# A decoder layer on one core: probability transposes by DMA instead of TensorE, in five pipeline stages

## The reference

```python
# self attention, on layernorm(x): q . (q @ anomaly) / sqrt(256)
scores = jnp.einsum('bsh,bth->bst', q, tq) / jnp.sqrt(jnp.float32(HIDDEN))
probs = jax.nn.softmax(scores, axis=-1)
ctx = jnp.einsum('bst,bth->bsh', probs, v)
return ctx * input_norm
# cross attention, on layernorm of the sum so far
attn = jnp.einsum('bhnd,bhmd->bhnm', q, k) * SCALE
attn = jnp.where(mask[:, None, :, :], attn, -jnp.inf)
attn = jax.nn.softmax(attn, axis=-1)
out = jnp.einsum('bhnm,bhmd->bhnd', attn, v)
# experts: idx = argmax(x @ Wg + bg); y = gelu(x @ W1[idx] + b1[idx]) @ W2[idx] + b2[idx]
```

## Time and profile before

| | us |
|---|---|
| median of 3 runs | 844.0 (843.88 to 845.4) |
| span of the profiled execution | 848.8 |
| TensorE, VectorE, ScalarE, GpSimd busy | 755.1, 653.2, 457.9, 138.9 |
| first and last x1 (start) | 115.0, 610.9 |
| experts' first matmul (start) | 706.8 |

### The profile page before, as it was taken

How to read it: one execution, slowest core, us unless ns; L and a number is a source line. 1 busy time by engine, 2 the same in 40 slices (tenths; PEclk the granted TensorE clock), 3 DMA queues, 4 the chain that set the end, 5 groups by cost and what they waited for, 6 DMA issues and landing times. The chain is left out here.

```text
span 848.8 us, 19493 instructions
## 1 busy us (share of the span) xinstructions
PE 755.1 (89%) x6136; PEld 681.1 (80%) x6137; DVE 653.2 (77%) x1619; ACT 457.9 (54%) x922; POOL 138.9 (16%) x246
## 2 busy tenths in 40 slices
PE   3988799999999999999999999999986416999996
PEld 2778689989889899898898998988975314999995
DVE  5984647788888888888888888888878465777773
ACT  2544626566566665666666656666665432334332
POOL 3100110120211201202112012021120410222221
PEclk9999989999999999999999999999978856999999
DMA  6242110010101000000010000000123260111110
GB/s 211 70 138 70 47 29 7 24 29 15 29 12 28 28 6 28 24 16 28 12 28 28 6 28 24 17 28 12 54 113 99 101 235 26 36 39 39 37 33 15
DMA packets 25525, 39.32 MB, mean 46 GB/s; under 512 B 3086, under 2 KB 18704, under 8 KB 25360
## 3 DMA queue, kind: packets, MB, share of 16 engines
q1 hardware_dynamic: 23232, 33.02, 12.5%
q0 software_dynamic: 2256, 5.83, 2.0%
HBM read 28.82 MB, written 10.41 MB: 46 GB/s over the span
## 5 line engine op out<-in xcount | busy, mean ns | idle before, releaser
L1076 ACT ACTIVATE ps_cross<-flip 128x512 f16<-128x512 f32 (+1 forms) x256 | 125.0, 514 | 116.5 <-PE flip L795 91.0
L1318 DVE TENSOR_TENSOR ps_cross<-flip,ps_cross 128x512 f16<-128x512 f32 (+1 forms) x256 | 145.0, 583 | 24.8 <-ACT ps_cross L1076 20.4
L795 PE MATMUL flip<-ident,exp_cross 128*128 128x128 f32 (+1 forms) x832 | 131.8, 282 | 9.9 <-DVE ps_cross L1318 6.5
L1277 ACT ACTIVATE exp_cross<-exp_cross,xneg 128x1024 f32<-128x1024 f32 (+1 forms) x128 | 122.7, 960 | 19.2 <-DVE xneg L1492 19.1
L784 PE MATMUL scores<-keys_cross,qt 128*128 128x402 f32 x512 | 127.6, 372 | 5.3 <-DVE xneg L1492 3.5
L795 PEld LDWEIGHTS flip<-ident,exp_cross 128*128 128x128 f32 (+1 forms) x832 | 95.8, 143 | 18.1 <-DVE ps_cross L1318 8.3
L672 PE MATMUL scores<-keys_self,u_tile 128*128 128x512 f32 x384 | 102.2, 403 | 6.4 <-issue 4.9
L806 PE MATMUL cross_out<-vals_cross,ps_cross 128*128 128x128 f16 (+1 forms) x832 | 102.5, 224 | 5.5 <-issue 4.9
L771 PE MATMUL flip<-vals_self,ps_self 128*128 128x256 f32 x768 | 103.8, 289 | 0.0
L806 PEld LDWEIGHTS cross_out<-vals_cross,ps_cross 128*128 128x128 f16 (+1 forms) x832 | 76.4, 101 | 28.3 <-issue 20.4
L771 PEld LDWEIGHTS flip<-vals_self,ps_self 128*128 128x128 f32 x768 | 96.7, 194 | 0.0
(11 more groups left out here) (207 smaller groups left out, 1189.2 us busy)
## 6 DMA issues: line engine op xcount, KB each, us to landing
w_stage<-W SPq DMA_DIRECT2D x8, 1024.0 KB, 5.4
u_dram<-u_out SPq DMA_DIRECT2D x4, 1024.0 KB, 5.9
u_tile<-u_dram SPq DMA_DIRECT2D x16, 256.0 KB, 2.7
mask_tile<-mask SPq DMA_DIRECT2D x16, 200.1 KB, 2.4
rows<-rows_dram SPq DMA_DIRECT2D x19, 130.0 KB, 2.1
x_all<-x SPq DMA_DIRECT2D x4, 512.0 KB, 5.8
x_tile<-x SPq DMA_DIRECT2D x16, 128.0 KB, 2.0
b_row<-b SPq DMA_DIRECT2D x1, 2048.0 KB, 8.9
```

What stands on the lines that cost most here:

```text
L795: tr = pe.transpose(flip[0:rows, bank(use), n * P:(n + 1) * P], exp_cross[:, h % 2, m * P:m * P + rows], ident[:, :])
L1076: return act.activation(out, in_, ACT.Copy, **kw)
L1277: act.activation(exp_cross[:, h % 2, cols], exp_cross[:, h % 2, cols], ACT.Exp, bias=xneg[:, h % 2, 1:2], scale=-1.0, accum_out=xden[:, ha ...
L1318: return dve.tensor_tensor(out, full, hi, ALU.subtract)
```

## The change

All float32 pieces that TensorE turned are now turned by DMA in their two float16 parts. The high part (`cross_hi`, `self_hi`) is made by ScalarE in SBUF before the turn, the low part in SBUF too: for cross heads 2, 3 and 0 on GpSimd (`low_cross`), for head 1 and both self halves on VectorE. SyncE issues 8 transposes of 128x1664 (416 KB) and 4 of 128x1024 (256 KB) per tile, 4352 KB together. The loop has five stages (`stages(k)`) and runs for j = 0 to 19: `a` is self scores of tile j, `s` self values, x1 and queries of tile j-1, `b` cross scores of tile j-2, `c` its later values and output (as j-3), `d` gate, rank and store of tile j-4. Self scores keep their four banks; cross scores use `flip` banks 0 and 1, one half head at a time; all small products share bank 2 (`SMALL`). The self values are float16 with a scale (`self_v`), the cross keys one copy with the queries in two parts, the mask's bias is made in two halves, and the expert weights are loaded and split in passes T to T+3.

```diff
+    def stages(k):
+        return k < T, 1 <= k <= T, 2 <= k <= T + 1, 3 <= k <= T + 2, k >= 4
...
+        def turn_cross(t, h, part):
+            if part == 0:
+                sp.wait_ge(cross_p_hi, H * t + h + 1)
+            else:
+                sp.wait_ge(cross_p_lo[h], t + 1)
+            sp.dma_start_transpose(out=cross_pt[:, h, part, :, :], in_=cross_p[:, h % 2, part, :]).wait_op(
+                constants_set, CONSTANTS, "sem-ge").then_inc(cross_turned[h], 16)
...
+        def body(j, k):
+            a, s, b, c, d = stages(k)
+            if c:
+                for h in (2, 3):
+                    for part in range(2):
+                        turn_cross(j - 3, h, part)
...
+            if b:
+                for h in (0, 1):
+                    for part in range(2):
+                        turn_cross(j - 2, h, part)
...
+            if a:
+                for half in range(2):
+                    for part in range(2):
+                        turn_self(j, k, half, part)
...
+        def low_cross(t, h):
+            pool.wait_ge(cross_p_hi, H * t + h + 1)
+            pool.tensor_tensor(cross_p[:, h % 2, 1, 0:MP], exp_cross[:, h % 2, :], cross_p[:, h % 2, 0, 0:MP],
+                               ALU.subtract).then_inc(cross_p_lo[h], 1)
...
-        def self_flip(j, k, g):
...
-                tr = pe.transpose(flip[:, bank(use), n * P:(n + 1) * P], exp_self[:, m * P:(m + 1) * P], ident[:, :])
...
+        def self_values(j, k, half):
+            pe.wait_ge(self_turned[half], 32 * j)
...
+            if half:
+                pe.wait_ge(cross_max_half, H * t + h + 1)
+            elif h or k > 2:
+                pe.wait_ge(cross_max_ready, H * t + h)
...
-        def cross_flip(j, k, h, g):
...
+        def cross_values(t, first, h):
+            pe.wait_ge(cross_turned[h], 32 * (t + 1))
...
+        def cross_hi(t, first, h):
...
+            copy(cross_p[:, h % 2, 0, 0:MP], exp_cross[:, h % 2, :]).then_inc(cross_p_hi, 1)
...
+        def cross_lo(t, h):
+            dve.wait_ge(cross_p_hi, H * t + h + 1)
+            low(cross_p[:, h % 2, 1, 0:MP], exp_cross[:, h % 2, :], cross_p[:, h % 2, 0, 0:MP]).then_inc(cross_p_lo[h], 1)
...
+            low(self_p[:, 1, at], exp_self[:, at], self_p[:, 0, at]).then_inc(self_p_lo, 1)
...
+                if h >= 2:
+                    dve.wait_ge(cross_p_lo[h - 2], t + 1)
+                elif k > 2:
+                    dve.wait_ge(cross_p_lo[h + 2], t)
...
-            if k == T:
-                weights_lo(0)
...
+            if k == T + 1:
+                weights_lo(0)
...
+            if k == T + 2:
                 weights_lo(2)
+                weights_lo(3)
...
+            if k == T + 3:
+                weights_lo(4)
+                weights_lo(5)
```

More of the change, by code:

```diff
@@ L44 @@
 V_TOP = 4096.0
-XHALF = 2 * 512
+SELF_V_TOP = 32768.0
+SELF_P_TOP = 16384.0
 RING = 4
 NOBODY = 65536.0
-NG = -(-MC // 4)
-XG = [range(4 * g, min(4 * g + 4, MC)) for g in range(NG)]
-BANKS = {("x", 2, 2): 0, ("x", 2, 3): 1, ("xn",): 2, ("x", 3, 0): 0, ("xq",): 2, ("qs",): 2,
[4 rows of a table removed]
[L64 to L70, removed]
+SMALL = 2
+PW = MC * P
+EARLY = 5
+STAGES = 4
 def build(nc, io):
@@ L465, in _, with turn_self, loads_w @@
         loads_a(0)
-        loads_x(0)
         sp.wait_ge(prologue_done, 3)
[L469 to L486, removed]
+        def turn_cross(t, h, part):
[5 more added lines that the diff above has]
+                constants_set, CONSTANTS, "sem-ge").then_inc(cross_turned[h], 16)
+        def turn_self(j, k, half, part):
+            at = slice(half * N // 2, (half + 1) * N // 2)
+            to = slice(half * T // 2, (half + 1) * T // 2)
+            sp.wait_ge(self_p_lo if part else self_p_hi, 2 * j + half + 1)
+            if k >= 1 and part == 0:
+                sp.wait_ge(self_p_used, 2 * j)
+            sp.dma_start_transpose(out=self_pt[:, part, to, :], in_=self_p[:, part, at]).wait_op(
+                constants_set, CONSTANTS, "sem-ge").then_inc(self_turned[half], 16)
+        def loads_w(n):
             e = n % E
@@ L798, in cross_values @@
-        def cross_values(j, k, h, g):
-            t = j - (2 if (h, g) in ((2, 0), (2, 1)) else stage_of(("x", h, g)))
-            pe.wait_ge(cross_p_lo, 16 * t + 4 * h + g + 1)
-            if h == 0 and g == 0 and k >= 2:
-                pe.wait_ge(o_summed, t)
-            for n, m in enumerate(XG[g]):
-                rows = P if m < MC - 1 else MLAST
-                pe.matmul(cross_out[:, h * P:(h + 1) * P], ps_cross[0:rows, g, 0, n * P:(n + 1) * P],
+        def cross_values(t, first, h):
+            pe.wait_ge(cross_turned[h], 32 * (t + 1))
+            if h == 0 and not first:
+                pe.wait_ge(o_summed, t)
+            for m in range(MC):
+                rows = P if m < MC - 1 else MLAST
+                pe.matmul(cross_out[:, h * P:(h + 1) * P], cross_pt[0:rows, h, 0, m, :],
@@ L995, in body @@
-            if c:
-                pe.wait_ge(x3t_ready, j - 1)
-                small(("gate",), j, k, x3t_ready, j - 1, gate_ready, gate)
+            if s:
+                small(xt_lo, j, q_ready,
+                      lambda out: three(out[:, 0:D], lambda a, c: xt[:, a, c, :], lambda b, c: wq_cross[:, b, c, :]))
+            if b:
+                cross_values(j - 2, k == 2, 0)
+            if c:
+                if s:
+                    pe.wait_ge(q_copied, j)
+                elif d:
+                    pe.wait_ge(rank_used, j - 3)
+                small(o_ready, j - 2, o_flipped, flip_row(o_tile[:, :, :].rearrange("p h d -> p (h d)")))
@@ L1025, in _ @@
+            if c:
+                if s:
+                    pe.wait_ge(qt_lo, j)
+                small(ot_lo, j - 2, wo_ready,
+                      lambda out: three(out[:, 0:D], lambda a, c: ot[:, a, c, :], lambda b, c: wo_cross[:, b, c, :]))
         run_pipeline(pe, body)
@@ L1521, in body @@
+            if d:
+                destination(j, k)
             if a:
@@ L1646, in body @@
[L1646 to L1655 removed]
+            if k == T + 2:
+                weights_lo(2)
+                weights_lo(3)
```

813 lines of the change are left out of this document (347 added, 466 removed), and 4 rows, old and new, of the table BANKS.

## The result

The changed kernel takes 928.5 us (median; 927.84 to 929.91) against 843.96 for the kernel before: 1.100 times as long, 95% interval 1.0975 to 1.1026. The forecast was 908 (848 to 980), slower.

What follows compares the result with a forecast made beforehand. A cycle through VectorE, GpSimd and TensorE was taken to set the changed loop's period at 35.5 us. In us: 848.8 + 7 (first x1) + 19 (loop) + 20 (tail) + 18 (clock) - 4.8 (offset) = 908, range 848 to 980.

Steps and rivals of the forecast that it cites:

- The cycle's steps: Loop: seven steps in line from one tile's x1 to the next, 34.8 us, or 35.5 with subtractions at 3.3.
- Step 2: Loop: VectorE's run up to cross_max of (3, 0), including cross_lo of head 1 and output work, 7.7 us.
- Step 5: Loop: GpSimd's power, mask half, subtractions of heads 2 and 3, copies and norm_col, 8.5 us with 3.07 per subtraction.
- The clock's term: Loop: TensorE's lowered clock in front of waiting engines costs 1.2 us per tile, 18 for 15 gaps; 0 to 40.
- steps 3 and 7: Loop: next scores and ScalarE's qt copy, 1.7 us; scores of (1, 0), 24 self values and hand-over, 3.8 us.
- 19 + 18: Loop: gaps of 21, 32.5 and 13 times 35.5 us, less 495.9, give 19; the lower clock adds 18.
- The prologue's term: Before the loop: first x1 about 7 us later, behind high and low parts, two transposes and all 48 values.
- The tail's term: After the last x1: one more stage, about 10 us, and the experts' weights' split, some 10; together 20.
- The offset: Whole kernel: 4.8 us subtracted because the profiled span stood that much above the median.
- The rival "faster": Loop: subtraction near 1.54 us and blocked steps falling beside others; 820 us for the kernel, chance 0.13.
- step 4: Loop: qt low, three small ones, two self_lo, cross_max (3, 1) and record's four operations, 5.7 us.
- that rival: Loop: GpSimd's subtraction at 4.2 to 5.0 us, or cross_lo and self_lo held too; 950 to 985 us, chance 0.11.

Runs made afterwards that it cites:

- run 1: The changed kernel with its three low_cross subtractions moved from GpSimd to VectorE, each ahead of the cross_max that waits for it: 896.3 us, 1.061.
- run 2: The changed kernel with GpSimd's three subtractions covering 402 of 1608 columns: 870.5 us, 1.031.
- run 5: The changed kernel with only the high parts turned, 6 DMA transposes per tile instead of 12: 918.9 us, 1.087.
- run 3: The changed kernel with gates parts 1 and 2 placed after cross_max (1, 0) in VectorE's order: 921.2 us, 1.091.
- run 6: The changed kernel with the prologue's GpSimd partition_all_reduce replaced by a memset of a fixed bound: 918.2 us, 1.087.
- kernel 8: The changed kernel with run 6's memset, new orders on VectorE and TensorE, and all three subtractions on VectorE: 822.9 us, 0.975.
- run 10: kernel 8 with only the high parts turned, 6 of 12 DMA transposes per tile: 817.6 us, 0.969.
- run 11: kernel 8 with the subtraction of head 3 back on GpSimd, those of heads 2 and 0 on VectorE: 831.5 us, 0.984.
- kernel 7: kernel 8's memset and new orders on VectorE and TensorE, but with the three subtractions on GpSimd: 907.0 us, 1.073.

## Why the prediction was right, and which terms were off

- **The cause** was the one forecast: a cycle through VectorE, GpSimd and TensorE, not the work of one engine. Run 1 moves GpSimd's part to VectorE, which was busier already, run 2 shortens it, and they gain 32 and 58 us; run 5 takes away half of the transposes and gains 2 of 538 us in the loop. That the time came out within the range is in part luck, as the terms show.
- **The cycle's steps**, predicted with 3.3 us for a subtraction and measured from 446.24: 1, 5.2 and 5.3 (to 451.54); 2, 7.7 and 8.4 (to 459.91); 3, 1.7 and 1.7; 4, 5.7 and 5.7 (to 467.34); 5, 9.0 and 9.6 (to 476.98); 6, 2.4 and 2.5 (to 479.51); 7, 3.8 and 4.0. The sum is 37.3 instead of 35.5. Step 2 was mis-sized: `xn` was not in it as held. It ends at 451.70, two small operations of the rank stand behind it, and so `cross_max` (2, 0) starts at 452.04, 0.5 us after GpSimd's subtraction. Step 5 has hand-overs and 0.39 us of waiting for ScalarE's copy.
- **GpSimd's subtraction**, taken as 3.3, is 3.26 us. The Trainium skill ("GPSIMD Engine Reference") gave 3.53 by an estimate; the row is 8% below.
- **The clock's term** of 18 us was wrong in its cause. The clock did fall to 0.51, but in steps 4 and 5, beside GpSimd's chain; steps 3 and 7, which the term was for, ran at 1.00 in the tile shown (459.91 to 461.64 and 479.51 to 483.50), and tiles at 0.86 and 0.95 took the same 37.26. Run 3 shows that this holds for this kernel's chain only: there the low clock fell on TensorE's part and cost up to 1.8 us in a tile.
- **The loop** came out at +42.5 against 19 + 18 = 37, and that is errors that meet: next to no clock, but 13 full gaps of 37.1 instead of 35.5 (+20.5) and a second gap of 35.5 instead of 32.5 (+3).
- **The prologue's term** was 7 and measured 15.8. Left out was the GpSimd reduction (8.6 of them, run 6); the other 7.2 are the size that the text had counted, though its items were not measured one by one.
- **The tail's term** of 20 measured 19.7, but its two halves (one stage more, the weights' split) were not measured, and they can't be all of it: the stretch of 115.6 us falls to 107.4 when the subtractions leave GpSimd (run 1) and to 103.0 in kernel 8, which has the same stages and the same split. That hit was in part luck.
- **The offset**, -4.8 between span and median, did not carry over: the changed kernel's median is 2.4 above its span. Its own profiled execution took 927.84 us with a span of 926.1; the span of 848.8 before was thus of an execution slower than the median of 844.0. That is 7.2 us of the 20.5 missed; the prologue is 8.8 and the loop 5.5, the tail and the blocks of the experts take 1.0 back.
- **The transposes** were taken at 24 us of the queue's time per tile and measured some 23 (run 5; with the loads 26, 0.71 of 37.3). That they lie beside was right.
- **The rival "faster"** asked for full gaps under 30.4 to 31.8 and said that VectorE and TensorE allowed it. Kernel 8 reached 30.9 and 822.9 us, near the 820 named, but by another order and not by a cheap GpSimd.
- **Slips in the working**, none of which moves the forecast: 13 gaps shorter by 7.9 us are 103 us, not 120; step 4's items add up to 5.9, not 5.7 (it measured 5.7); and a subtraction of 4.2 to 5.0 us alone gives 943 to 974, so that the 950 to 985 of that rival needs held operations too.

What stays open: which chain sets kernel 8's 30.6 us, since no engine is full, half of the transposes (run 10) and 1.7 us of VectorE's work (run 11) gave nothing; what the low clock costs there, where a tile at 0.95 takes 31.28 us and one at 1.00 takes 30.56, but which of the two brings the other isn't shown; and whether a better order on ScalarE would take more off, which was not tried.

## What to carry to other kernels

Moving work off a busy engine is worth only what the longest chain through the waits gets shorter: here TensorE lost some 7.5 us per tile (33.4 before, 25.9 in kernel 8, both at clock 1.00) and the full gap grew by 3.1, because small steps stood in line behind long ones on an engine that was busy less than half of the time. Look for long elementwise work on GpSimd with VectorE operations beside it, count those as held, and try such work on VectorE, right ahead of what waits for it, before judging the rest of the change. A new pipeline wants its order tuned as a whole: order and place gave 11 and 32 us apart, and 95 together. And a low clock has a price only where TensorE is what the chain waits for: nothing in the changed kernel's tiles shown, up to 1.8 us per tile in run 3.

## What the runs showed of the hardware

- GpSimd's work holds VectorE operations with one tensor input too, not only those with two: `xn` (128x256, one tensor and two columns of scalars, 0.42 us in the kernel before) took 2.30 in the changed kernel and 3.18 in kernel 7 (3.3 in all tiles but the first). The Trainium skill ("SBUF — State Buffer") calls the port pair shared between these two engines an exclusive lock, which these rows bear out.
- It works the other way as well. In kernel 8 GpSimd's copy of 128x256, 0.40 us else, reads 1.87 us beside VectorE's subtraction:

```profile
375.46 1.88 DVE L1208 TENSOR_TENSOR cross_p<-exp_cross,cross_p 128x1608 f16<-128x1608 f32 x1
375.73 1.87 POOL L640 COPY x_older<-x_old 128x256 f32<-128x256 f32 x1
```

- VectorE's `cross_max`, which reads PSUM and one SBUF tensor, was held nowhere: 0.98 to 1.06 us in all kernels, and 1.05 in run 3 where it ran (398.36 to 399.41) within GpSimd's subtraction (396.78 to 400.03).
- A partition reduction on GpSimd that shows 0.38 us kept work that was ready at 17.12 waiting until 25.19, and the first x1 by 8.6 us.
- A DMA transpose of 128x1664 in 2 bytes lands after 4.0 us in the median, of 128x1024 after 3.3 (issues with KB, if uniform, and us to landing, of the changed kernel):

```profile
cross_pt<-cross_p SPq DMA_TRANSPOSE x128, 4.0
...
self_pt<-self_p SPq DMA_TRANSPOSE x64, 3.3
```
